# Values added to their bias in two bank-sized halves, and a denominator that waits for each half at its own bank

## What is computed

```python
emb = x + pos_encod                       # x: normalised input
q, k, v = emb @ wq + bq, emb @ wk + bk, emb @ wv + bv
w   = pos_bias * (abs(i - j) < 64)
ek  = exp(k - max_k);  ew = exp(w - max_w)
num = einsum('tj,bjd->btd', ew, ek * v)
den = einsum('tj,bjd->btd', ew, ek)
a   = layer_norm(sigmoid(q) * num / den @ wo + bo + emb)
y   = layer_norm(relu(a @ w1 + b1) @ w2 + b2 + a)
x   = x + tanh(g) * y
```

## Time and profile before

| | |
|---|---|
| median of 3 runs | 451.56 us (451.43 to 451.65) |
| the profiled execution | 450.98 us, span 449.3 us |
| TensorE busy (PE) | 433.1 us, 96% of the span, 2892 matmuls |
| weight loads (PEld) | 393.4 us, 88% |
| VectorE (DVE) | 378.6 us, 84%, 769 instructions |
| ScalarE (ACT) | 286.9 us, 64% |
| GpSimd (POOL) | 291.8 us, 65% |
| chain that ended last | POOL 26%, issue 21%, PE 17%, DVE 10%, ACT 2%, DMA 1% |

### The profile page before, as it was taken

One profiled execution on the slowest core, in us unless ns is written; L12 is line 12 of the kernel. 1 busy time (PEld: TensorE's weight loads), 2 busy tenths in 40 slices (PEclk: granted clock), 3 DMA queues, 4 the chain that ended last, 5 costly groups with the idle time before them and its releaser, 6 DMA issues.

```text
span 449.3 us, 8151 instructions
## 1 busy us (share of the span) xinstructions
PE 433.1 (96%) x2892; PEld 393.4 (88%) x2892; DVE 378.6 (84%) x769; ACT 286.9 (64%) x453; POOL 291.8 (65%) x230
## 2 busy tenths in 40 slices
PE   8999999999979999999999999999999999999995
PEld 7888798889869888898989888998989998998985
DVE  5898878989778979799797979799788877679877
ACT  3682654848475578745977477745976387629373
POOL 3766856554768557894778647895677543783642
PEclk9999999999989999999999999999999999999999
DMA  8840420451234750448215661436313331011002
GB/s 283 282 140 4 134 76 2 140 150 52 93 98 139 199 141 1 140 126 216 93 49 161 187 151 31 142 101 193 96 42 100 104 103 39 1 48 47 3 0 95
DMA packets 43498, 47.23 MB, mean 105 GB/s; under 512 B 8513, under 2 KB 39745, under 8 KB 43457
## 3 DMA queue, kind: packets, MB, share of 16 engines
q1 hardware_dynamic: 42368, 45.13, 33.4%
q10 hardware_dynamic: 1088, 1.57, 1.0%
HBM read 30.76 MB, written 15.93 MB: 104 GB/s over the span
## 4 chain that ended last, share of the span: by engine, by line
POOL 26%; issue 21%; PE 17%; DVE 10%; ACT 2%; DMA 1%; SPq 0%; POOLq 0%; ACTq 0%; DVEq 0%
PE ps L1855 17%; POOL ek_lo L242 4%; POOL ev_lo L242 3%; POOL x_beta L650 3%; DVE hid_lo L1147 3%; POOL emb L354 2%; POOL xk_lo L242 2%; POOL a_rows L650 1%; DVE xk L1070 1%; POOL rs_fin L630 1%; POOL rs_ff L630 1%; POOL nmr_fin L633 1%; POOL rs_mid L630 1%; POOL ve_ff L621 1%; DVE xk L922 1%
## 5 line engine op out<-in xcount | busy, mean ns | idle before, releaser
L1855 PE MATMUL ps<-w_hi,hid_hi 128*128 128x256 f32 x248 | 61.0, 282 | 0.0
L1855 PE MATMUL ps<-w_lo,hid_hi 128*128 128x256 f32 x248 | 60.8, 282 | 0.0
L1630 ACT ACTIVATE hid_hi<-ps,b 128x512 fp32r<-128x512 f32 x60 | 37.7, 680 | 23.1 <-PE ps L1855 23.0
L1855 PE MATMUL ps<-a_hi,w_hi 128*128 128x512 f32 x128 | 50.8, 397 | 0.0
L1855 PE MATMUL ps<-a_hi,w_lo 128*128 128x512 f32 x128 | 50.7, 396 | 0.0
L242 POOL TENSOR_TENSOR ek_lo<-y,ek_hi 128x1024 fp32r<-128x1024 f32 x13 | 36.2, 2782 | 21.3 <-DVE xr L1070 17.5
L1855 PEld LDWEIGHTS ps<-w_hi,hid_hi 128*128 128x128 f32 x248 | 46.7, 188 | 0.6 <-issue 0.2
L1855 PEld LDWEIGHTS ps<-w_lo,hid_hi 128*128 128x128 f32 x248 | 46.7, 188 | 0.3
L1147 DVE SCALAR_TENSOR_TENSOR hid_lo<-ps,neg_b,hid 128x512 fp32r<-128x512 f32 x60 | 41.3, 737 | 3.3 <-ACT hid L1636 3.2
L1636 ACT ACTIVATE hid<-hid_hi,neg_b 128x512 f32<-128x512 f32 x60 | 40.0, 722 | 0.0
L1855 PE MATMUL ps<-w_hi,hid_lo 128*128 128x256 f32 x248 | 36.0, 285 | 1.0 <-DVE hid_lo L1147 0.4
(11 more groups left out here) (287 smaller groups left out, 1414.5 us busy)
## 6 DMA issues: line engine op xcount, KB each, us to landing
x_in<-in_x SPq DMA_DIRECT2D x8, 512.0 KB, 4.7
emb<-in_ctx SPq DMA_DIRECT2D x8, 512.0 KB, 4.0
x_beta<-in_x SPq DMA_DIRECT2D x8, 512.0 KB, 4.4
out<-out_sb SPq DMA_DIRECT2D x7, 512.0 KB, 4.4
key_room<-norm SPq DMA_DIRECT2D x6, 512.0 KB, 2.6
y<-key_room SPq DMA_DIRECT2D x24, 128.0 KB, 2.9
fin_room<-xk SPq DMA_DIRECT2D x6, 512.0 KB, 2.6
out_sb<-fin_room SPq DMA_DIRECT2D x24, 128.0 KB, 2.9
```

The source lines that it names most:

```text
L1630: act.activation(tile(hi, b, T), bank(relu_pair(n, q), b), ACT.Relu, bias=b1[:, m:m + 1]).then_inc(hid_hi_done, 1)
L1855: return pe.matmul(o, s, m, start=start, stop=stop, skip_group_check=True)
```

## The change

`keep_values` takes the values out with two instructions of half the size, one for each bank of the pair, and each signals `val_done`. All counts of `val_done` double. TensorE's `step` waits for the first half (`2 * i + 1`) before the denominator's bank 0, and inside `weigh`, for the denominator alone (`part == 0`), for the second half (`2 * n + 2`) before bank 1. `weigh_values` and the waits of the first two sequences still want both halves.

```diff
@@ keep_values
-                bv = bv_rows.rearrange("p (o d) -> p o d", o=1).to_broadcast([P, TT, D])
-                dve.tensor_tensor(val.rearrange("p (a d) -> p a d", a=TT), pair(src).rearrange("p (a d) -> p a d", a=TT),
-                                  bv, ALU.add).then_inc(val_done, 1)
+                bv = bv_rows.rearrange("p (o d) -> p o d", o=1).to_broadcast([P, TT // 2, D])
+                for h in range(2):
+                    dve.tensor_tensor(half(val, h).rearrange("p (a d) -> p a d", a=TT // 2),
+                                      bank(src, h).rearrange("p (a d) -> p a d", a=TT // 2), bv, ALU.add
+                                      ).then_inc(val_done, 1)
@@ weigh_values
-                dve.wait_ge(val_done, n + 1)
+                dve.wait_ge(val_done, 2 * (n + 1))
@@ weigh, before near(dst, 1, ...)
+                if part == 0:
+                    pe.wait_ge(val_done, 2 * n + 2)
@@ TensorE, before weigh_first() and before add_hidden(0, 0)
-            pe.wait_ge(val_done, 1)
+            pe.wait_ge(val_done, 2)
-            pe.wait_ge(val_done, 2)
+            pe.wait_ge(val_done, 4)
@@ TensorE's step
-                pe.wait_ge(val_done, i + 1)
+                pe.wait_ge(val_done, 2 * i + 1)
```

## The result

| | before | after |
|---|---|---|
| median | 451.49 us (6 runs, 450.93 to 451.65) | 447.51 us (6 runs, 447.40 to 447.75) |
| ratio | | 0.9913, 95% interval 0.9899 to 0.9928 |
| the profiled execution | 450.98 us, span 449.3 | 447.75 us, span 446.0 |

The change makes the kernel faster, by 3.9 us (3.3 to 4.6 by the interval). I had forecast faster, by the mechanism that the trace shows, but 448.7 us with 448.1 as the low end. So the question for the experiments was double: is the mechanism the cause, and which term was too small.

What follows compares the result with a forecast made beforehand. The chain from GpSimd's nmr_fin through hid_lo into TensorE was taken as the bound. Gains of 3.1 us over steps 2 to 5, less 0.2 at the start, gave 451.56 - 2.9 = 448.7 us; range 448.1 to 452.2.

Steps and rivals of the forecast that it cites:

- The bound: The chain from GpSimd's nmr_fin over ScalarE's norm, transposes and hid_lo into TensorE at 216.23 sets the pace.
- TensorE's 0.46 (part 2): TensorE's denominator starts 0.46 us earlier on the first half; worth zero, as it waits for hid_lo later.
- The exchange of the port (part 3): nmr_fin starts 0.08 before weigh_values, gets the port and ends at 209.94 instead of 211.01; chance 0.70.
- The row that spoke against the rule: At 96.70 VectorE led by 0.04, yet GpSimd's ve_ff was not held up (0.20).
- The split (part 1): Two 128x512 copies in keep_values instead of one make what follows on VectorE start 0.09 us later.
- The slower rival: keep_values halves do not overlap, 0.2 at each of six places: +1.2, 452.8 us; chance 0.06.
- What the exchange gives (part 4): Numerator starts earlier by 0.4, 1.3, 2.2 and 3.1 us after the exchanges of steps 2 to 5.
- first term: Transposes, hid_lo and TensorE's numerator start 0.4 us earlier after nmr_fin is quick.
- The second term: GpSimd's emb ends earlier, so VectorE's first xk is no longer held: 0.5 us a step.
- TensorE's room: TensorE's three stands, 0.46 + 0.3 + 0.26 = 1.0 a step, leave room for 0.9.
- The start (part 5): At 57.90 and 98.49 the split copy delays the chain by 0.1 us each, 0.2 in all.
- Step 6 adds nothing: After 319.09 TensorE runs 57 us without a stand, so the exchange in step 6 gains nothing.

Runs made afterwards that it cites:

- Halves with one wait: Changed kernel, but TensorE waits for both halves before the denominator's bank 0 and the wait inside the denominator is gone; 447.47 us, ratio 0.9922.
- the added write: Kernel before, plus a 59 ns VectorE write of one spare column between sums_low and weigh_values in steps 2 to 6; 447.50 us, ratio 0.9921.
- the later start of `x_beta`: Changed kernel plus one GpSimd pow of 128x2 (0.70 us) ahead of x_beta in steps 2 to 6; 446.71 us, ratio 0.9897.
- the port given back: Changed kernel plus one 128x4 GpSimd instruction (0.20 us) ahead of nmr_fin in steps 2 to 6; 451.42 us, ratio 1.0006.

## Why the prediction was right, and where it failed

**The bound, and TensorE's 0.46 (part 2): right.** Halves with one wait cost nothing; the early wait without the port gains nothing.

**The exchange of the port (part 3): right in all five places.** I gave it 0.70 and asked if a lead of 0.08 would do. It was 0.06 here and 0.10 with the added write, and each time enough; the other way 0.01 and 0.09 were enough for VectorE. The row that spoke against the rule, is no accident. The same pair of instructions meets twice in each of the fourteen traces, VectorE 0.04 ahead by its record every time, and `ve_ff` takes 0.20 in all 28. VectorE pays instead: its `x` takes 0.52 in these 28 places and at most 0.49 in its 364 others. All 28 `x` of the kernel before, two of them in this place, ns least, median and most:

```profile
L1016 DVE SCALAR_TENSOR_TENSOR x<-res,mv_ff,gamma_t x28: 471/478/516, 96.7 to 404.4; 128x256 f32<-128x256 f32 x28
```

So the start in the record is not quite the moment that decides: `weigh_values` wins with 0.01, this instruction loses with 0.04. The two are of different kinds (this one also reads one number per partition); which part of that matters was not tested.

**The split (part 1): 0.06, taken as 0.09.** A half lasts 0.66 to 0.69, and the second starts 0.57 to 0.61 behind the first, so they overlap by some 0.08. The slower rival needed 0.15.

**What the exchange gives (part 4): the step that failed, by the size of its first term.** I let VectorE's `norm` start at 211.08, 0.03 after the end of `weigh_values` at 211.05, and took 0.4. The trace shows 0.55 to 0.56. An instruction that waits for nobody starts before its predecessor's record ends: `norm` at 210.30, `weigh_values` until 210.38. That is 0.11, and 0.03 comes from the cheaper split. The second term was 0.5 and measured 0.48. So a step gives 1.03 instead of 0.9, and 0.55 + 3 x 1.03 = 3.64 instead of 3.1: 0.54 of what the forecast was short of. The start, below, is another 0.2.

**TensorE's room, from which I took the low end of the range: made of the wrong pieces, and no bound.** I had added three stands, 0.46 + 0.3 + 0.26 = 1.0. The start distances of TensorE's matmuls over one step, summed by kind, show what went: 0.45 at the denominator, 0.31 at the first `hid_lo`, 0.12 by which the matmuls behind these two started late, and 0.15 at two places of `w_hi,ev_lo` that I had not looked at (0.1 at 242.51). That is 1.03, so the sum of 1.0 came near by luck. The 0.26 at the numerator stayed, and the later start of `x_beta` took 0.4 a step more. So 0.4 + 3 x 1.0 - 0.2 = 3.2 was no bound. The range ended at 448.1 where the measured terms, from 451.56, give 447.9.

**The start (part 5): 0.2, and nothing like it is seen.** The values of step 2 start at 156.69 and 156.56 in two kernels with the split start, at 156.62 before, and the version without the split is not faster. It is at most 0.1.

**The base.** I subtracted from 451.56, the median of three runs. The kernel before has 451.11 to 451.49 in the later comparisons, so up to 0.4 of the 1.2 us can lie there. From the 451.49 that the change was compared with, the measured terms give 447.85, 0.34 above the 447.51 that was measured. The interval of the gain (3.3 to 4.6) holds both, and what the 0.34 is stays open. The two profiled executions differ by 3.23, or by 3.6 without the 0.37 of the start.

**Step 6 adds nothing: right** (+0.14, interval -0.23 to +0.54).

## What to carry to other kernels

Where VectorE and GpSimd run beside each other on SBUF, look for one instruction with two very different durations in the trace, and read who started first: a lead of 0.06 us decided between 0.20 and 1.27. Compare only like with like: another pair of instructions turned at a different lead. A change that moves a start by a tenth of a microsecond can be worth more than what it was made for, and can also undo it; an order by design did the same here with one short instruction (447.50) as the split that happened to bring it (447.51), and it can be used at a second place too (446.66). When the gain per step is read off a chain, let an instruction that waits for nobody start before its predecessor's end, and take what an engine can still gain from all its start distances over a step, not from the stands that one view names.

## What the runs showed of the hardware beyond that

The held instruction's end follows the holder's end by a fixed time of its own, whatever its start: `nmr_fin` 0.06 after `weigh_values` (211.01 and 210.95; 211.08 and 211.02 with the port given back), the first `xk` 0.55 after `emb` in all 30 places where it was held, over eight kernels. An `xk` that starts 0.08 to 0.17 before `emb` ends takes its plain 0.74 and loses nothing. I read this as the first part of an instruction going on without the port; no run separates that from other readings. The Trainium skill, "SBUF — State Buffer", section "SBUF: two separate sides", says that whichever of the two starts first keeps the shared ports for its whole length; in the three places that were followed here (`nmr_fin`, `xk`, `out_sb`) the traces agree, down to leads of 0.01 and 0.06 us. In the place of the earlier trace rows they don't, by the starts in the records. That the thing held is a port comes from the skill; the traces show only who holds whom, and until when.

Chains of such holds exist: `x_beta` holds `out_sb`, which then holds `ek_lo` (3.4 instead of 2.4). When the first order changes, the others do too.

The time that a load takes can turn such an order: GpSimd's `emb` waited 0.4 to 0.9 for `in_ctx` at 288 to 298 us in six of the fourteen traces and not in the others. In the kernel before and its relatives this made the step shorter (51.03 to 51.19 instead of 51.42), in the fastest versions it made it longer. In the changed kernel with `x_beta` late:

```profile
290.13 2.42 POOL L355 TENSOR_TENSOR emb<-x_in,emb 128x1024 f32<-128x1024 f32 x1 [0.68 <-DMA emb<-in_ctx]
```

and the distance is 51.07 there, 50.0 in the steps beside it. An earlier load of `in_ctx` would be the next thing to try; it wasn't tried.
